# Masks level by level, weight splits at tick ends, the last fed tile earlier, and the closing sums ahead of the last tile

## The reference

```python
x = x + attn(layernorm(x))
#   q, k, v = silu(causal_conv4(xn @ W));  q, k normalised per head;  beta = sigmoid(xn @ Wb)
#   per chunk of 64 tokens: A = (K*beta) K^T;  T = inverse of (I + tril(A, -1));  W = T Kb;  U = T Vb
#   scan over chunks with a state S;  o = o * rsqrt(mean(o*o)) * g;  out = o @ Wo
y = layernorm(x)
#   scores = sigmoid(y @ centroids.T);  top 2 of 8 by sigmoid(raw + bias);  weights = softmax of the two scores
x = x + y + sum_shared gelu(y Wfc) Wproj + sum_top2 w * gelu(y Wfc_r) Wproj_r
```

## Time and profile before

| | |
|---|---|
| median of 3 runs | 1236.01 us (1230.71, 1236.01, 1236.26) |
| profiled execution | 1232.95 us, its span 1231.2 us |
| granted PE clock, mean | 0.962 |
| PE busy | 1114.2 us (90%) |
| PE weight loads busy | 959.5 us (78%) |
| DVE busy | 694.7 us (56%) |
| ACT busy | 622.5 us (51%) |
| POOL busy | 365.0 us (30%) |
| chain that ended last | PE 65%, DVE 11%, issue 11%, ACT 6%, POOL 5%, DMA 2% |

### The profile page before, as it was taken

How to read it: one execution, slowest core, us unless ns; L and a number is a source line. 1 busy time by engine, 2 the same in 40 slices (tenths; PEclk the granted TensorE clock), 3 DMA queues, 4 the chain that set the end, 5 groups by cost and what they waited for, 6 DMA issues and landing times.

```text
span 1231.2 us, 25608 instructions
## 1 busy us (share of the span) xinstructions
PE 1114.2 (90%) x9320; PEld 959.5 (78%) x9321; DVE 694.7 (56%) x1211; ACT 622.5 (51%) x1117; POOL 365.0 (30%) x320
## 2 busy tenths in 40 slices
PE   4596889999999998877988989999999999999996
PEld 1464768787878787766877878898999998999996
DVE  4667857676767675575689642333333333333377
ACT  4565556756565655355633643444444444444442
POOL 0415343424252425122011112334334334333100
PEclk9698879999999999998999989999999999999998
DMA  3202020202020102253222421111111111111456
GB/s 131 69 18 69 1 77 1 78 10 78 10 78 10 61 10 95 78 156 112 95 86 78 138 61 57 43 50 52 43 51 49 45 51 47 47 51 51 145 197 230
DMA packets 54088, 86.36 MB, mean 70 GB/s; under 512 B 6656, under 2 KB 39296, under 8 KB 53888
## 3 DMA queue, kind: packets, MB, share of 16 engines
q1 hardware_dynamic: 46336, 64.37, 16.2%
q0 software_dynamic: 7680, 20.98, 5.5%
HBM read 60.16 MB, written 25.17 MB: 69 GB/s over the span
## 4 chain that ended last, share of the span: by engine, by line
PE 65%; DVE 11%; issue 11%; ACT 6%; POOL 5%; DMA 2%; SPq 0%; DVEq 0%; ACTq 0%; POOLq 0%
PE ps L1398 25%; PE ps L1378 22%; PE ps L1232 4%; PE ps L1389 3%; PE ps L1222 2%; PE ps L1297 2%; POOL W L823 2%; PE ps L1456 2%; POOL W L842 2%; PE ps L1304 1%; ACT W L1071 1%; DVE late_room L1749 1%; PE ps L1358 1%; DVE W L1560 1%; DVE W L1652 1%
## 5 line engine op out<-in xcount | busy, mean ns | idle before, releaser
L1378 PE MATMUL ps<-late_room,W 128*128 128x256 f16 x3072 | 352.9, 273 | 28.5 <-DVE late_room L1749 22.6
L1398 PE MATMUL ps<-W,late_room 128*128 (+1 forms) x3264 | 373.2, 274 | 0.3 <-DVE late_room L1749 0.3
L1378 PEld LDWEIGHTS ps<-late_room,W 128*128 (+1 forms) x3072 | 298.6, 98 | 70.4 <-DVE late_room L1749 28.5
L1398 PEld LDWEIGHTS ps<-W,late_room 128*128 128x128 f16 x3264 | 321.7, 99 | 40.4 <-DVE late_room L1749 0.5
L1097 ACT ACTIVATE ps<-ps 128x512 f32<-128x512 f32 x272 | 158.6, 583 | 354.5 <-PE ps L1378 316.8
L1749 DVE SCALAR_TENSOR_TENSOR late_room<-ps,late_room 128x512 f16<-128x512 f32 x272 | 181.0, 687 | 233.4 <-ACT late_room L1102 233.4
L1102 ACT ACTIVATE late_room<-ps 128x512 f16<-128x512 f32 x272 | 155.7, 595 | 2.5
L1560 DVE SCALAR_TENSOR_TENSOR W<-W 128x512 f32<-128x512 f32 x144 | 109.1, 758 | 10.2 <-ACT W L959 6.8
L940 ACT COPY W<-ps 128x512 f32<-128x512 f32 x112 | 61.5, 589 | 86.7 <-PE ps L1297 70.4
L1232 PE MATMUL ps<-W 128*128 128x512 f16 x384 | 97.3, 399 | 7.1 <-DVE W L1575 3.8
L1997 DVE TENSOR_SCALAR late_room<-ps 128x512 f32<-128x512 f32 x36 | 24.9, 691 | 97.7 <-PE ps L1398 97.7
(11 more groups left out here) (188 smaller groups left out, 1372.1 us busy)
## 6 DMA issues: line engine op xcount, KB each, us to landing
wstage<-in_w_ffn SPq DMA_DIRECT2D x40, 512.0 KB, 3.8
W<-yt_d SPq DMA_DIRECT2D x16, 512.0 KB, 5.8
late_room<-in_x SPq DMA_DIRECT2D x8, 512.0 KB, 4.6
W<-in_x SPq DMA_DIRECT2D x8, 512.0 KB, 4.1
x2n_d<-W SPq DMA_DIRECT2D x8, 512.0 KB, 3.1
base_d<-W SPq DMA_DIRECT2D x8, 512.0 KB, 3.6
late_room<-base_d SPq DMA_DIRECT2D x16, 256.0 KB, 4.2
acc_d<-late_room SPq DMA_DIRECT2D x12, 256.0 KB, 2.2
```

The costliest lines, as they stand in the source:

```text
L1378: last = pe.matmul(up_bank(n, c)[:, f * XT:(f + 1) * XT], weight(slot, d, hw, cols), x_halves[:, hx, d], start=(q == 0), stop=(q == len(pa ...
L1398: last = pe.matmul(down_bank(b)[:, c * D:(c + 1) * D], hs[b][:, hh, f, c * P:(c + 1) * P], weight(slot, DB + f // 4, hw, cols), start=(q = ...
```

## The change

- The masks are waited for one by one: Y_s of level s waits for product s only. `AT` moves into the first half of `KbT`, so ACT's copy no longer waits for the last level of the group before but for DVE's `edges_kept`; and ACT's squares, which share that room, wait for all masks of the group before.
- The multiplication of Q's edges (L1600) moves from slot 14 of `front` to slot 6 of `back`, one tick later.
- The weight splits move: two at slot 12 of tick 1, one at slot 6 and two at slot 12 of tick 2, the same again in tick 3. The last two pieces are loaded later.
- The last fed tile (n = 6): its first four up pieces go to slots 2 and 3 of tick 10, two a slot, in PSUM banks 0 to 3; its other four to slots 8 to 11; its first two down parts to slots 12 and 14 of tick 10, the others to slot 1 of tick 11. The tile before it (n = 5) has its first two down parts together in slot 1.
- DVE's low half of the first early tile (`x_low_half`) stands inside `router(0)`, behind its first two operations.
- The sums: each unit's `acc` blocks are combined before that unit's `y_shared`; the last final tile gets its expert rows added to its base two units ahead; nothing is combined behind the last `y_shared`.

```diff
@@ -149,8 +149,25 @@
...
 AHEAD_FILLS = [(f"xnT{d}", "dve") for d in range(DB)]
-DOWN_SLOTS = {1: (0, 0), 3: (0, 1), 5: (1, 0), 6: (1, 1)}
-UP_SLOT = SLOTS_A - 4 * N_SH
+DOWN_SLOTS = {1: ((0, 0),), 3: ((0, 1),), 5: ((1, 0),), 6: ((1, 1),)}
+DOWN_SLOTS_TAIL = {1: ((0, 0), (0, 1)), 5: ((1, 0),), 6: ((1, 1),)}
+Y_SLOTS = {3: 0, 6: 1}
+UP_SLOTS = {SLOTS_A - 4 * N_SH + 4 * e + c: ((e, c),) for e in range(N_SH) for c in range(4)}
+UP_SLOTS_TAIL = {2: ((0, 0), (0, 1)), 3: ((0, 2), (0, 3)), 8: ((1, 0),), 9: ((1, 1),), 10: ((1, 2),), 11: ((1, 3),)}
+DOWN_SLOTS_LAST = {1: ((1, 0), (1, 1))}
+DOWNS_AHEAD = {12: (0, 0), 14: (0, 1)}
+def downs(slot, n):
+    return {FED - 2: DOWN_SLOTS_TAIL, FED - 1: DOWN_SLOTS_LAST}.get(n, DOWN_SLOTS).get(slot, ())
+def ups(slot, n):
+    return (UP_SLOTS_TAIL if n == FED - 1 else UP_SLOTS).get(slot, ())
 class Tile:
@@ -270,19 +287,11 @@
...
 assert G_ROUTED % 2 == 0 and R_TILES % 2 == 0
-SUM_UNITS = range(2, N_SH * FINAL + 1)
-PER_SUM = G_ROUTED // (len(SUM_UNITS) - 1)
-assert PER_SUM * (len(SUM_UNITS) - 1) == G_ROUTED
-def sums_at(u):
-    own = [("final", u // N_SH - 1)] if u % N_SH == 0 else []
-    kept = range(PER_SUM * (u - 2), min(PER_SUM * (u - 1), G_ROUTED))
-    return own + [("acc", q) for q in kept]
-SUMS = [s for u in SUM_UNITS for s in sums_at(u)]
+SUMS_AT = {2: [("acc", 0), ("acc", 1), ("final", 0)], 3: [("acc", 2), ("acc", 3)], 4: [("acc", 4), ("acc", 5), ("final", 1)],
+           5: [("acc", 6), ("acc", 7), ("ahead", 3)], 6: [("acc", 8), ("acc", 9), ("final", 2)], 7: [("acc", 10), ("acc", 11)]}
+SUM_UNITS = range(2, N_SH * FINAL)
+SUMS = [s for u in SUM_UNITS for s in SUMS_AT[u]]
+assert FINAL == 4 and G_ROUTED == 12 and len(SUMS) == FINAL + G_ROUTED
 def sum_rows(s):
@@ -313,7 +322,7 @@
...
                 extra(slot, t)
-SPLIT_AT = [(8, 1), (9, 1), (13, 1), (14, 1), (8, 2), (9, 2), (13, 2), (14, 2)]
+SPLIT_AT = [(12, 1), (12, 1), (6, 2), (12, 2), (12, 2), (6, 3), (12, 3), (12, 3)]
@@ -432,7 +441,7 @@
...
         Y, room = carve(arena, CONST_ROOM, (GT, P))
-        AT = Y
+        AT = KbT[:, 0].rearrange("p (k t) -> p k t", k=GT)
         XTr, room = carve(arena, room, (GT, P))
@@ -586,11 +595,11 @@
...
         turn_bank = ps[:, 4, :]
-        assert XB == 2 and SLOTS_A - UP_SLOT == 4 * N_SH
+        assert XB == 2
         def up_bank(n, c):
-            return ps[:, 5 + c % 2, :] if isinstance(n, int) and n < U_EARLY else ps[:, c, :]
+            return ps[:, 5 + c % 2, :] if isinstance(n, int) and n < U_EARLY - N_SH else ps[:, c, :]
         def down_bank(b):
@@ -662,9 +671,10 @@
...
             load_ahead(2)
-            for p in range(4, SH_PIECES):
+            for p in range(4, SH_PIECES - 2):
                 load_shared_piece(p)
             load_ahead(3)
+            load_shared_piece(SH_PIECES - 2)
             def load_base(t):
@@ -706,6 +716,8 @@
...
                 sp.dma_start(xr, tokens(x, n)).then_inc(xr_in[b], 16)
+                if not n:
+                    load_shared_piece(SH_PIECES - 1)
                 if n == GROUPS - 1:
@@ -775,6 +787,11 @@
...
                 kind, v = s
+                if kind == "ahead":
+                    sp.wait_ge(y_out, final_tile(v).unit(N_SH - 1) + 1)
+                    sp.dma_start(rows_of(out, sum_rows(s)), yo[final_tile(v).par]).then_inc(y_stored[final_tile(v).par], 16)
+                    return
                 sums, done = (acc[v], acc_out) if kind == "acc" else (yo[final_tile(v).par], y_stored[final_tile(v).par])
@@ -785,12 +802,14 @@
...
             for u in SUM_UNITS:
-                for s in sums_at(u):
-                    store_sums(s)
+                for s in SUMS_AT[u]:
+                    if s[0] != "ahead":
+                        store_sums(s)
                 if u + 2 in SUM_UNITS:
...
                     load_base(final_tile(u // N_SH + 1))
+            store_sums(("ahead", FINAL - 1))
             sp.wait_ge(acc_out, 16 * len(ACC_ROWS))
@@ -948,6 +967,9 @@
...
                     if m in (2, 3):
+                        if m == 2 and n:
+                            act.wait_ge(masked, (LEVELS - 1) * n)
                         act.wait_ge(silu_done, 3 * DB * n + i + 1)
@@ -1015,12 +1037,13 @@
...
                     act.wait_ge(*fr.full(n, "AT"))
-                    if n:
-                        act.wait_ge(*bk.full(n - 1, f"Z{LEVELS - 1}"))
+                    act.wait_ge(edges_kept, 2 * (n + 1))
                     act.copy(AT.rearrange("p k t -> p (k t)"), fr.bank("AT")).then_inc(at_kept, 1)
...
                     act.wait_ge(*fr.full(n, "edges"))
+                    if n:
+                        act.wait_ge(q_edges, n)
                     kept_edges = DB * GCH * (b + 1)
@@ -1288,9 +1310,8 @@
...
                     if slot % 2 == 0:
+                        pe.wait_ge(masked, (LEVELS - 1) * n + s)
                         if s == 1:
-                            pe.wait_ge(masked, (LEVELS - 1) * (n + 1))
                             pe.wait_ge(*fr.empty(n, "X"))
@@ -1399,16 +1420,37 @@
...
                 return last
+            def down_fed(n, e, c):
+                if c == 0:
+                    pe.wait_ge(h_low, 4 * N_SH * n + 4 * (e + 1) if n == FED - 1 else 4 * N_SH * n + 4 + 3 + e)
+                    if n == FED - 1:
+                        pe.wait_ge(y_out, N_SH * (n - 1) + e + 1)
+                last = down_part(e, c, e)
+                if c == XB - 1:
+                    last.then_inc(down_done, 1)
             def up_piece(slot, n, b):
-                if slot >= UP_SLOT:
-                    e, c = divmod(slot - UP_SLOT, 4)
+                if n == FED - 1 and slot in DOWNS_AHEAD:
+                    down_fed(n, *DOWNS_AHEAD[slot])
+                for e, c in ups(slot, n):
                     u = N_SH * n + e
-                    if slot == UP_SLOT:
+                    if (e, c) == (0, 0):
                         if not n:
...
                         pe.wait_ge(fed_low, n + 1)
-                    if e == 0 and c < 2 and n:
+                    if n == FED - 1:
+                        if e == 0:
+                            ring, kept_act, kept_dve = (fr, "X", "AT") if c < 2 else (bk, f"XT{LEVELS - 2}", f"Z{LEVELS - 1}")
+                            pe.wait_ge(*ring.empty(GROUPS - 1, kept_act))
+                            pe.wait_ge(*ring.empty(GROUPS - 1, kept_dve))
+                        else:
+                            pe.wait_ge(h_low, 4 * (u - 1) + c + 1)
+                    elif e == 0 and c < 2 and n:
                         pe.wait_ge(y_out, N_SH * (n - 1) + c + 1)
@@ -1417,14 +1459,8 @@
...
             def down_piece(slot, n, b):
-                if slot in DOWN_SLOTS:
-                    e, c = DOWN_SLOTS[slot]
-                    if c == 0:
-                        pe.wait_ge(h_low, 4 * N_SH * n + 4 + 3 + e)
-                    last = down_part(e, c, e)
-                    if c == XB - 1:
-                        last.then_inc(down_done, 1)
+                for e, c in downs(slot, n):
+                    down_fed(n, e, c)
             def rank_rows():
@@ -1594,15 +1633,15 @@
...
                     dve.tensor_tensor(XTr, XTr, idt[:].unsqueeze(1).to_broadcast([P, GT, P]), ALU.add).then_inc(x0t_ready, 1)
-                if slot == 14:
+            def flat(a):
+                return a.rearrange("p k t -> p (k t)")
+            def back(slot, n, b):
+                if slot == 6:
                     dve.wait_ge(enorm, n + 1)
...
                     dve.tensor_tensor(edge(QT[b], b), edge(QT[b], b), rn, ALU.mult).then_inc(q_edges, 1)
-            def flat(a):
-                return a.rearrange("p k t -> p (k t)")
-            def back(slot, n, b):
                 if slot < 10 and slot % 2:
@@ -1767,13 +1806,12 @@
...
             def up_piece(slot, n, b):
-                if slot >= UP_SLOT:
-                    e, c = divmod(slot - UP_SLOT, 4)
+                for e, c in ups(slot, n):
                     low(N_SH * n + e, e, c)
             def down_piece(slot, n, b):
-                if slot in DOWN_SLOTS and DOWN_SLOTS[slot][1] == XB - 1:
-                    y_shared(fed_tile(n), DOWN_SLOTS[slot][0])
+                if slot in Y_SLOTS:
+                    y_shared(fed_tile(n), Y_SLOTS[slot])
             def split_piece(slot, t):
@@ -1808,6 +1846,11 @@
...
             count = rank_bank[:, TTOK * N_RT:2 * TTOK * N_RT].rearrange("p (t e) -> p t e", e=N_RT)
+            def x_low_half(t):
+                dve.wait_ge(x_high, t.turn + 1)
+                hi, lo = (xs[t.par][:, q].rearrange("p d t -> p (d t)") for q in range(2))
+                dve.scalar_tensor_tensor(lo, turn_bank, X_SCALE, hi, ALU.mult, ALU.subtract).then_inc(x_low, 1)
             def router(part):
@@ -1816,6 +1859,7 @@
...
                     then(dve.memset(r["onec"], 1.0))
+                    x_low_half(early_tile(0))
                     dve.wait_ge(scored, 2)
@@ -1978,14 +2025,18 @@
...
                     v, e = divmod(u, N_SH)
```

(15 more changed lines are left out.)

21 lines of the change are left out of this document (12 added, 9 removed).

## The result

The changed kernel took 1218.74 us (median of 4 runs, 1216.28 to 1221.28), the kernel before 1233.36 in the same session: ratio 0.9888, 95% interval 0.9852 to 0.9923. Run again later, in another session, it took 1222.03 (7 runs, 1215.62 to 1223.99) beside 1231.89: 0.991, 0.9879 to 0.9941. All 11 runs together have the median 1221.3. So it is faster, by some 10 to 15 us or 0.9 to 1.1%, and the forecast of 1221 (1213 to 1229) holds. The profiled execution took 1221.28 with a span of 1219.5, that is 11.7 less than the profiled execution of before.

What follows compares the result with a forecast made beforehand. PE was taken as busy for 94% of full ticks, leaving three stretches where it stands. Fill -4.9, last fed tile -4.4 and end -4.4 sum to -13.7: 1219.3 from the profiled execution, 1222.3 by the median; forecast 1221, range 1213 to 1229.

Steps and rivals of the forecast that it cites:

- Tick 1, -4.8: Fill, tick 1: Y1 waits for one mask and X, starting at 52.65 instead of 57.44; gain 4.8 us.
- Tick 2 cancels: Fill, tick 2: a removed split and the new slot 6 split cancel; first X at 97.2 instead of 97.44.
- The clock term: Ticks 2 and 3: low clock behind new PE pauses, about 1.5 and 1 us; 0.7 charged after halving and offsets.
- the rival that called slot 6 a poor place: Fill gives back its gain through DVE's wait and PE's low clock; fill worth 0.4 to 1, 1225.5; chance 0.14.
- DVE's reduction, -3.7: Fill, before tick 3: L1652 at 115.67 moves up 2.7 to 5.1 us, bounded by POOL's L838; 3.7 taken.
- The fill's sum, -4.9: Ticks 1 to 3 together: -4.8 - 3.7 + 2.4 + 0.5 + 0.7 = -4.9 us; ends -7.5 and -0.4.
- The full ticks take it over unchanged.: Full ticks pass on the fill's gain, since each begins when the one before ends; 64.6 us apart as now.
- the prediction's own sign: Full ticks: the forecast is wrong if they change their length from 64.6 us apart.
- Last fed tile, -4.4: Tick 10 to router(1): PE gains 5.8 us, but DVE's busy queue passes on 4.4; L1694 2.8 us late.
- Q's edges in full ticks, 0: Full ticks: DVE's 2.6 us wait at slot 14 goes, PE unaffected; value 0, at most 0.3 a tick.
- End, -4.4: After the last low half: fewer DVE sums, last store 4.5 us earlier, 4.4 taken; ends -5.2 and +1.
- The slower rival: Eight ticks: ACT's squares wait for all masks; POOL beyond 4.6 us late stalls ACT, above 1242; chance 0.04.

Runs made afterwards that it cites:

- e7: Changed kernel with DVE's multiplication of Q's edges back in slot 14 of `front`; 1228.13 us, 0.9968 of the kernel before.
- e2: Changed kernel with the slot 6 splits of ticks 2 and 3 moved to slot 4; 1214.45 us, 0.9856 of the kernel before.
- e10: Changed kernel with POOL's power of the edges moved behind the next tick's product of V; 1216.96 us, 0.9875 of the kernel before.
- e6: Changed kernel with the first level product waiting for all five masks again; 1224.37 us, 0.9947 of the kernel before.
- e4: Changed kernel with the last fed tile's slots and the first early tile's low half of x as before; 1221.84 us, 0.9911 of the kernel before.
- e9: The changed kernel timed again, nothing altered; 1222.03 us, 0.9910 of the kernel before.
- e5: Changed kernel with only the first early tile's low half of x put back behind the router's first part; 1226.37 us, 0.9956 of the kernel before.
- e1: Changed kernel with the end's sums placed as before; 1223.96 us, 0.9947 of the kernel before.
- e3: Changed kernel with unused words around Kb's room, so A's copy starts on a 64-byte multiple; 1215.26 us, 0.9863 of the kernel before.
- e12: e8 with the room of masks and CT also on a 64-byte multiple; 1214.31 us, 0.9854 of the kernel before.
- e8: Changed kernel with the edits of e2, e3 and e10 together; 1210.61 us, 0.9840 of the kernel before.

## Why the prediction was right, step by step

The sum was -13.7 on the profiled execution; that pair of traces gives -11.7, and the medians of the two sessions -9.9 and -14.6. The three main terms (fill, last fed tile, end) came out within 1 us each in that pair of traces. The terms:

- *Tick 1, -4.8.* Y1 moved by 4.2, to 53.28 for 52.65. Right. But this gain rests on the move of Q's edges, which the term didn't say: e7 has Y1 at 53.17 and 0.6 us of it left at tick 2's first X.
- *Tick 2 cancels.* The first X of tick 2 is 4.1 earlier, no more than tick 1 gave: right as a sum. But the parts were larger than priced. The split at slot 6 cost DVE's addition 2.4 us (2.7 were worked out), and the clock behind the pause another 2.5 (2.04 and 3.48 for 1.05 and 1.95), where "I charge half of it less what the removed waits give back: 0.7" stood. The clock term was mis-sized. Delay and clock of both splits were priced at 2.7 + 2.4 + 0.7 = 5.8 us in all, and e2 gives 6.8 by the medians; the rival that called slot 6 a poor place had its mechanism right, though not its sum.
- *DVE's reduction, -3.7.* It moved from 115.67 to 107.58, 8.1 with tick 1's share; 8.5 was forecast. It does stand behind POOL's product, as said, but that this bounds tick 3 is only part of it: with the product freed, DVE's own queue holds the reduction to 106.29, only 1.3 us earlier (e10).
- *The fill's sum, -4.9.* -4.0 at tick 4. It is a small balance of larger parts, which depend on each other and don't simply add up: e7 and e6 put Q's edges at 8 us and the single waits at 5, e2 the splits of slot 6 at 7 against them. That it fits within 1 us is in part luck, the more so as the same fill came out up to 5 us shorter in e4.
- *"The full ticks take it over unchanged."* Not quite: 1.5 us lost by the slower masks. No step had priced the new place of A's copy, and the prediction's own sign, "wrong if full ticks change their length", came true by 0.17 to 0.67 us a tick; it was too small to move the sum out of its range. Tick 9 gave 1.6 back in this pair (a wait of 2.67 us ahead of L1318 for 3.84), by luck: in e9, the same kernel, that wait is 4.49 and tick 9 takes 56.47 us for 53.65.
- *Last fed tile, -4.4.* -4.4 between tick 10 and router(1), and the 2.8 us of delay of L1694's successor was there too (17.71 us into tick 10 for 14.95). "This and not PE's 5.8 is what reaches the routed tiles" is shown by e5. Then 1.7 us went into the slow third product, which no term had; it is the clock's, not the tile's.
- *Q's edges in full ticks, 0.* Right for the full ticks. In the fill its worth was inside the -3.7 of DVE's reduction ("That wait goes") and had no line for tick 1; e7 gives it 8.2 us in all (6.8 by the medians), the largest single piece of the change.
- *End, -4.4.* -5.0, by trace and e1. The base was waited for 0.58 us (DVE at 1201.22), far from the 3 us that would have broken the term. The prediction counted 28 operations on sums behind the last low half before; there are 24. The slip touched nothing, since its sum is built on the 20 that remain.

The marks came near: the first late product is 9.8 us earlier (10 to 11 announced), router(1) 8.5 (9 to 10), since 1.5 us of the fill's gain was lost on the way. The slower rival, ACT's squares behind the masks, showed nowhere: the full ticks from 5 on are 64.65 to 66.31 us long, before 64.48 to 66.14.

## What to carry to other kernels

An operation put into a slot of an in-order queue is paid for by the pause of whoever waits behind it, and a pause on PE is often paid twice, since what follows can run at the lower clock (in eight of nine traces behind the 2.7 us here); look for the idle stretch of both engines that it needs (slot 4 here) before choosing a slot. When a buffer is given another home to save a wait, compare the duration of every operation that reads it before and after. And two edits can be worth something only together, as the single waits and Q's edges are in tick 1: take back each alone before crediting either. Look at several traces of one kernel before a stretch of one of them is given to an edit.

## What the runs showed of the hardware

*The same fill runs 5 us apart with the clock.* e4 has the changed kernel's fill, instruction for instruction. Clock of 80 to 90 us (stretch, length, PE's busy time, granted clock), changed and then e4, and PE of e4 behind the same pause:

```profile
80.00:90.00 10.00, 6.57 (x34) 0.68 0.18 52
```

```profile
80.00:90.00 10.00, 5.96 (x48) 1.00 0.18 52
```

```profile
81.53 1.13 PE L1318 MATMUL ps<-W 128*128 128x128 f32 x8 [2.71 <-issue]
...
84.86 2.05 PE L1291 MATMUL ps<-W 128*128 128x128 f32 x16
```

A pause of 2.71 us left the clock at its upper level (2.4 GHz) in the one execution; 2.70 was followed by the lower one (1.2 GHz) in the other. That place makes 2.7 us of difference, up to the next first X. Two more make up the rest: tick 1, where Y1 ran 1.13 us in e4 and 2.04 in the changed kernel (1.2), and the output projection L1361 of tick 3, 3.63 and 5.30 (1.7, of which 0.3 is lost again elsewhere). Tick 4 began at 154.84 and 160.16. That is as large as the terms of this change. Runs of one kernel spread over 8 us (1215.62 to 1223.99 for the changed one), and the fastest of them shows the highest mean clock (0.971, the others 0.963 to 0.970); that such falls are all of the spread isn't shown.

*POOL's time depends on where operands lie.* The same tensor_tensor of 128x512 f32 takes 1.09 or 1.27 us by shifts of its operands in the partition that differ by less than 64 bytes (e3 and e12, above).

*Pairs on the port.* Five masks took 7.62 us in tick 2 of the changed kernel beside DVE's splits, 5.73 in e3 and e8; a full tick's five take 6.18 and 5.28. So the two splits cost POOL 1.4 us in the one and 0.5 in the others, not the 2.5 of their own length, which the prediction had weighed as an end. It took that from a rule of the Trainium skill, "SBUF — State Buffer", on the shared port pair: by it DVE's reduction would have moved by 2.7 us beyond tick 1's gain; it moved by 3.9. The traces agree with the exclusion itself (DVE's L1756, on four elements a partition, takes 1.22 us beside a mask of 1.27, 1.04 beside one of 1.09, and 0.16 alone, at 525.04). Why the splits cost POOL less than their length isn't shown. For Y1 it didn't matter: in tick 1 they begin at 54.75, behind the first mask, which is all that Y1 waits for.
